# Two blocks instead of one ahead of the expert loop in the second mixture layer, with GpSimd making their low halves

## Chip, cores and metric

The kernel runs on one core of a Trainium2 chip. The metric is device time in microseconds (us): the median of the runs. Three runs of the kernel before took 1082.74, 1085.60 and 1086.61 us; the median is 1085.6 us.

## What is computed

A token matrix x (2048 x 256) passes four stages, each behind a layer norm and a residual with a tanh gate: cross attention, mixture of experts, quantised cross attention, mixture of experts. The change touches the last stage only. Cut to what matters:

```python
def _L1_ffn_ref(...):            # E, I, IS = (16, 176, 704), TOP_K = 4
    x = hidden_states.reshape(-1, h)                 # 2048 x 256
    w_dense = _routing_weights(x, router_w)          # softmax over 16 experts, the 4 best kept
    moe_out = _moe_experts(x, gate_w, up_w, down_w, w_dense)
    shared = jax.nn.silu(x @ shared_gate_w.T) * (x @ shared_up_w.T) @ shared_down_w.T
    shared = jax.nn.sigmoid(x @ se_gate_w.T) * shared
    return (moe_out + shared).reshape(b, s, h)
```

Every token goes through its four experts (the routed part) and through one shared expert of width 704 (the shared part). The two parts are independent until they are added.

## The kernel before

All engine queues are written out by hand, so the order of the work is the order of the program text on each engine, and semaphores alone tie the engines together (`s_h`, `s_hh` and so on; a wait is `at_least(engine, semaphore, base, n)`). `ffn_pe`, `ffn_act`, `ffn_dve` and `ffn_pool` hold one mixture layer's part of TensorE, ScalarE, VectorE and GpSimd; `l` is 0 for the first mixture layer and 1 for the second, which is the only one whose order changes.

**Shared work** is cut into 24 items (`NSH`): 4 blocks of 512 tokens (`BLK`), times 6 chunks of the inner width (`KSH`: five of 128 and one of 64). One item `s` is a chain over four engines: `shared_gate_up(s)` on TensorE (12 matmuls of 512 columns, 6 in the narrow chunk), `shared_silu` on ScalarE (L761), `shared_product` on VectorE (L839, into `wk1`), `shared_high` on ScalarE (L767, the fp16 high half, into `wkh`), `shared_low` on VectorE (L846, the fp16 rest: `wk1` minus `wkh`, into another part of `wkh`), `shared_down` on TensorE (L679, 12 matmuls of 256 columns). `shared_down(s-2)` stands behind `shared_gate_up(s)`. The six items of a block add up in two PSUM banks (4 and 5); `shared_out(b)` on VectorE (L815, four instructions) adds the block to `x_sb` and so frees the banks (`s_accr`).

**Where the items stand.** `HALF = KSH`, so in each mixture layer 6 items (block 0) stand ahead of the expert loop and 18 items (blocks 1 to 3) behind it. The ones ahead are interleaved, one per step `s`, with the routing: `route_part_dve` and `route_part_pe` do at step 0 to 3 the choice of an expert (`choose_dve`), then weights, bases, slots, then at steps 7 to 10 `rows_dve` (one-hot tables, L550, L551, L553), whose products `list_pe` (L386) adds up on TensorE one step later, and at step 12 `list_dve`, which writes the token numbers `ids` (L565, `r_ids`). With `ids` written, `ffn_pool` gathers the rows of 256 slots per group `g` by two indirect DMAs (L631), for 40 groups, at most four groups ahead (`XR`).

**Expert loop.** `group(base, s)` does one group of 256 slots per step on TensorE: transposes of the gathered rows (L703, into PSUM banks 4 and 5, the shared accumulators' banks, so they wait for `s_accr`), gate and up, a transpose, down. The output goes to a DRAM table `ys`.

**Behind the loop** GpSimd gathers for each of the 16 token tiles four rows of `ys` (`gather_rows`, L656: 64 indirect DMAs, at most four tiles ahead of `combine`, by `c_used`). VectorE's loop there has one step `i` per shared item: `shared_out` at `i` = 8, 14 and 20, `shared_product`, `shared_low`, and `combine(i-2)` (L825, L828), in this order. SyncE then stores each finished tile to `out`.

```python
            for s in range(max(HALF + 3, FIRST_STEPS[l])):
                if s == LIST_STEP[l] - 1:
                    shared_out(0)
                route_part_dve(dve, l, s)
                if s < HALF:
                    shared_product(s)
                if 1 <= s < HALF + 1:
                    shared_low(s - 1)
```

## Time and profile before

| | us |
|---|---|
| median of 3 runs (lowest, highest) | 1085.60 (1082.74, 1086.61) |
| the profiled execution's own time | 1080.46 |
| span of its trace | 1078.7 |
| TensorE busy in the span | 847.4 |
| VectorE busy | 751.3 |
| GpSimd busy | 644.2 |
| ScalarE busy | 460.8 |
| mean granted TensorE clock | 0.828 of full speed |

The span runs from the first to the last instruction; 1.8 us of the execution lie outside it. Positions below are us from the start of the span. In a row of the timeline the first number is the start, the second the duration (of several instructions with "x", from the first to the last), and the bracket behind it tells how long the engine had been idle and what ended that; "remote" there means that the releaser isn't seen. In the granted clock 1.00 is 2.4 GHz and 0.50 is 1.2 GHz.

### The profile page before, as it was taken

The page shows a single profiled execution, that of the slowest core. Times are in us where ns is not written, and L with a number is a line of the kernel's source. Part 1 is how long each engine was busy: PE and PEld are TensorE (multiplying, and loading weights), DVE is VectorE, ACT ScalarE, POOL GpSimd, SP SyncE. Part 2 cuts the span into 40 slices and gives each one's busy share as a digit, 9 for nine tenths or more (in the row PEclk, how much of TensorE's full clock was granted, in tenths as well). Part 3 has the DMA queues.
Part 4 walks back from the last instruction along what each step waited for, and adds up shares of the span by engine and source line. Part 5 has one row for each costly group of instructions (what it writes and reads, how often), then busy time and mean ns, then how long its engine had stood idle before and what let it go on. Part 6 is the DMA issues. An engine that isn't in the chain of part 4 may idle for free.

```text
span 1078.7 us, 21036 instructions
## 1 busy us (share of the span) xinstructions
PE 847.4 (79%) x6928; PEld 569.6 (53%) x6929; DVE 751.3 (70%) x1527; ACT 460.8 (43%) x993; POOL 644.2 (60%) x851
## 2 busy tenths in 40 slices
PE   4379667699989777777777787858679999993785
PEld 1267445477645445545445455545557777761442
DVE  5788668466576777798787787947847676751564
ACT  3455243233223356667656666824023333320121
POOL 4597780766285778888888887610054444426752
PEclk9699859799999866687787686758579999996887
DMA  7021142345221100000110000010034444423331
GB/s 250 26 79 40 47 132 57 97 138 158 94 81 49 47 22 11 12 22 22 28 53 13 16 4 2 2 57 22 6 97 127 136 125 136 126 87 99 113 96 56
DMA packets 55444, 75.04 MB, mean 70 GB/s; under 512 B 11068, under 2 KB 46656, under 8 KB 55360
## 3 DMA queue, kind: packets, MB, share of 16 engines
q1 hardware_dynamic: 44992, 44.82, 13.0%
q0 software_dynamic: 10368, 29.14, 10.0%
q8 instruction: 48, 0.79, 0.3%
q14 instruction: 36, 0.29, 0.1%
HBM read 51.45 MB, written 22.49 MB: 69 GB/s over the span
## 4 chain that ended last, share of the span: by engine, by line
PE 39%; POOL 16%; DVE 14%; issue 10%; ACT 6%; DVEq 5%; POOLq 4%; another core or an unknown queue 4%; DMA 2%; SPq 0%; ACTq 0%
PE PS L256 23%; PE PS L679 3%; DVE sb_slotv L1303 2%; PE PS L1188 2%; POOL sb_xnf L631 2%; POOL sb_wk L1606 2%; PE PS L703 2%; PE PS L732 2%; PE PS L1178 2%; ACT sb_wk L1262 1%; POOL sb_region L1412 1%; POOL sb_wkh L1606 1%; POOL sb_xnf L656 1%; PE PS L1099 1%
## 5 line engine op out<-in xcount | busy, mean ns | idle before, releaser
L631 POOL DMA_INDIRECT sb_xnf<-token_table,sb_ids x120 | 115.8, 965 | 181.3 <-DVE sb_ids L565 87.1
L256 PE MATMUL PS<-sb_region,sb_wkh 88*128 (+1 forms) x1440 | 210.8, 297 | 6.1 <-DVE sb_wa L886 2.9
L1303 DVE TENSOR_REDUCE sb_slotv<-PS 128x1 f32<-128x512 f32 x256 | 163.7, 681 | 44.3 <-PE PS L1178 44.3
L256 PEld LDWEIGHTS PS<-sb_region,sb_wkh 88*128 88x128 f16 (+1 forms) x1440 | 138.2, 99 | 57.0 <-issue 12.2
L656 POOL DMA_INDIRECT sb_xnf<-slot_table,sb_place x96 | 96.8, 1008 | 85.1 <-DMA slot_table<-sb_wa 39.2
L256 PE MATMUL PS<-sb_xnT,sb_sgu 128*128 128x512 f16 x528 | 131.5, 398 | 7.7 <-issue 6.5
L679 PE MATMUL PS<-sb_sdn,sb_wkh 128*128 128x256 f16 (+1 forms) x576 | 77.6, 288 | 42.9 <-DVE sb_wkh L846 34.2
L1262 ACT ACTIVATE sb_wk<-PS,sb_slotv 128x512 f32<-128x512 f32 x128 | 86.9, 686 | 37.3 <-DVE sb_slotv L1303 33.4
L761 ACT ACTIVATE sb_wk<-PS 128x512 f32<-128x512 f32 (+1 forms) x48 | 28.6, 596 | 172.0 <-PE PS L256 105.5
L679 PEld LDWEIGHTS PS<-sb_sdn,sb_wkh 128*128 128x128 f16 (+1 forms) x576 | 56.6, 102 | 68.2 <-DVE sb_wkh L846 43.3
L1606 POOL TENSOR_SCALAR sb_wk<-sb_wk 128x512 f32<-128x512 f32 x128 | 79.5, 621 | 21.4 <-ACT sb_wk L1262 12.6
L256 PEld LDWEIGHTS PS<-sb_xnT,sb_sgu 128*128 128x128 f16 x528 | 52.3, 101 | 72.2 <-issue 22.8
L839 DVE SCALAR_TENSOR_TENSOR sb_wk<-PS,sb_wk 128x512 f32<-128x512 f32 (+1 forms) x48 | 33.2, 692 | 80.4 <-ACT sb_wk L761 64.8
L1308 DVE TENSOR_SCALAR sb_wkh<-PS 128x1024 f16<-128x1024 f16 x112 | 76.6, 684 | 10.7 <-PE PS L1200 10.1
L780 ACT ACTIVATE sb_wkh<-PS 128x512 f16<-128x512 f32 x60 | 35.8, 597 | 109.7 <-PE PS L703 102.3
L875 DVE SCALAR_TENSOR_TENSOR sb_wk<-PS,sb_sm,sb_wk 128x176 f32<-128x176 f32 x120 | 42.6, 396 | 51.4 <-ACT sb_wk L789 47.7
L1188 PE MATMUL PS<-sb_idh,sb_wk 128*128 128x128 f16 x512 | 58.5, 269 | 10.6 <-DVE sb_wkh L1308 5.5
L859 DVE TENSOR_TENSOR sb_wkh<-PS,sb_wkh 128x512 f16<-128x512 f32 x60 | 41.4, 691 | 34.9 <-ACT sb_wkh L780 33.5
L789 ACT ACTIVATE sb_wk<-PS 128x352 f32<-128x352 f32 x60 | 27.8, 463 | 86.5 <-PE PS L256 73.1
L1188 PEld LDWEIGHTS PS<-sb_idh,sb_wk 128*128 128x128 f16 x512 | 39.6, 120 | 38.8 <-issue 31.5
L1262 ACT ACTIVATE sb_wkh<-PS,sb_slotv 128x512 f32<-128x512 f32 x64 | 43.4, 682 | 30.9 <-DVE sb_slotv L1303 29.1
L1412 POOL TENSOR_TENSOR sb_region<-sb_stg,sb_region 128x704 f16<-128x704 f32 (+1 forms) x32 | 43.5, 1359 | 20.8 <-issue 19.8
(281 smaller groups left out, 1808.3 us busy)
## 6 DMA issues: line engine op xcount, KB each, us to landing
slot_table<-sb_wa SPq DMA_DIRECT2D x60, 256.0 KB
sb_stg<-gu SPq DMA_DIRECT2D x24, 352.0 KB, 3.0
sb_stg<-dn SPq DMA_DIRECT2D x24, 176.0 KB
token_table<-sb_xnf SPq DMA_DIRECT2D x16, 256.0 KB, 3.7
sb_stg<-sgu SPq DMA_DIRECT2D x8, 352.0 KB, 6.5
sb_x_sb<-x SPq DMA_DIRECT2D x1, 2048.0 KB, 12.2
out<-sb_x_sb SPq DMA_DIRECT2D x16, 128.0 KB
sb_xnf<-token_table,sb_ids POOLq DMA_INDIRECT x120
```

The lines of the kernel that those rows point to most:

```text
L256: last = nc.tensor.matmul(out_, lhs(i, c), rhs(j, c), start=(c == 0 and n == 0 and not begun), stop=(c == C - 1 and n == 2 and not more))
L631: nc.gpsimd.indirect_dma_start(xg[l][:, 2 * (g % XR) + n, :], None, xw[l][:, :], bass.IndirectOffsetOnAxis(ap=ids[:, 2 * g + n:2 * g + n + ...
L656: nc.gpsimd.indirect_dma_start(yr[l][r][:, k, :], None, ys[l][:, :], bass.IndirectOffsetOnAxis(ap=place[:, k, t:t + 1], axis=0))\
L679: last = nc.tensor.matmul(PS[:, 4 + i // 2, i % 2 * D:(i % 2 + 1) * D], wkh[0:r, HR * h + v, i * P:(i + 1) * P], sdn[0:r, j, k, :], start= ...
L859: nc.vector.tensor_tensor(wkh[:, 2 * (s % 2) + 1, :], PS[:, 4 + s % 2, :], wkh[:, 2 * (s % 2), :], ALU.subtract).then_inc(e_xl[l].sem, 1)
L875: last = nc.vector.scalar_tensor_tensor(wk1[:, 2 + u, n * EI:(n + 1) * EI], PS[:, 2 * u + n, EI:EG], wv[u][:, n:n + 1], wk1[:, u, n * EI:( ...
L1188: last = nc.tensor.transpose(bank[:, (h * KT + k) * P:(h * KT + k + 1) * P], h_p[s % NE][:, h, k * P:(k + 1) * P], idh[:, :])
L1262: nc.scalar.activation(h_e[s % NE][:, h, :], PS[:, 2 * u + h, :], ACT.Exp, bias=h_nb[u][:, h:h + 1], accum_out=o_sum[v][:, head:head + 1]) ...
L1303: nc.vector.tensor_reduce(h_nb[u][:, h:h + 1], PS[:, 2 * u + h, :], AX, ALU.max, negate=True).then_inc(h_max, 1)
L1308: nc.vector.tensor_scalar(h_T[s % 2], PS[:, 4 + s % 2, :].bitcast(F16), -RB, None, ALU.add).then_inc(h_pc_dve, 1)
L1412: nc.gpsimd.tensor_tensor(lo, w, hi, ALU.subtract).then_inc(stg_split[n % 4], 1)
L1606: nc.gpsimd.tensor_scalar(h_e[s % NE][:, h], h_e[s % NE][:, h], 255.0, MAGIC + RB_BITS, ALU.mult, ALU.add).then_inc(h_int, 1)
```

## The change

`HALF` becomes a pair, `AHEAD = (KSH, 2 * KSH)`: the first mixture layer keeps 6 items ahead of its loop and 18 behind it, the second has 12 and 12. The second layer's routing loop runs 15 steps on VectorE and 14 on TensorE instead of 13. The first `shared_out` of that layer moves from step 11 to step 8, and a second one is added behind `list_dve`. The low halves of the 12 items ahead go from VectorE (L846) to GpSimd, with a semaphore of their own, `s_lowp`: ten ahead of the first gather, one behind the gathers of group 0, one behind those of group 1. VectorE's loop behind the expert loop is lengthened past its last item, so that the 16 combines fit.

```diff
-        HALF = KSH
+        AHEAD = (KSH, 2 * KSH)
...
+        s_lowp = sem("s_lowp")
...
         LIST_STEP = tuple(2 * k + 4 for k in TOPK)
-        FIRST_STEPS = tuple(max(HALF + 2, n + 1) for n in LIST_STEP)
+        OUT_STEP = (LIST_STEP[0] - 1, KSH + 2)
+        FIRST_STEPS = tuple(max(a + 2, n + 1) for a, n in zip(AHEAD, LIST_STEP))
...
+            def shared_low(s):
+                r = P if s % KSH < SFULL else SREM
+                at_least(pl, s_hh[l], 0, s + 1)
+                at_least(pl, s_d[l], 0, s + 1 - HR)
+                nc.gpsimd.tensor_tensor(wkh[0:r, HR + s % HR, :], wk1[0:r, 2 + s % 2, :], wkh[0:r, s % HR, :],
+                                        ALU.subtract).then_inc(s_lowp, 1)
+
             if l == 0:
                 split_items(pl, 0, FIRST_ITEMS)
+            else:
+                for s in range(AHEAD[1] - 2):
+                    shared_low(s)
             at_least(pl, r_ids[l], 0, 1)
...
             for g in range(NG[l]):
                 gather(g)
+                if l == 1 and g < 2:
+                    shared_low(AHEAD[1] - 2 + g)
...
-                at_least(pe, s_hl[l], 0, s + 1)
+                if l == 1 and s < AHEAD[1]:
+                    pe.wait_ge(s_lowp, s + 1)
+                else:
+                    at_least(pe, s_hl[l], 0, s + 1 - l * AHEAD[1])
...
-            at_least(pe, s_h[l], 0, HALF)
-            at_least(pe, s_accr[l], 0, HALF // KSH)
+            at_least(pe, s_h[l], 0, AHEAD[l])
+            at_least(pe, s_accr[l], 0, AHEAD[l] // KSH)
...
                 at_least(dve, s_silu[l], 0, s + 1)
                 at_least(dve, s_hh[l], 0, s - 1)
+                if l == 1 and 2 <= s < AHEAD[1] + 2:
+                    dve.wait_ge(s_lowp, s - 1)
...
-            for s in range(max(HALF + 3, FIRST_STEPS[l])):
-                if s == LIST_STEP[l] - 1:
+            for s in range(max(AHEAD[l] + 3, FIRST_STEPS[l])):
+                if s == OUT_STEP[l]:
                     shared_out(0)
                 route_part_dve(dve, l, s)
-                if s < HALF:
+                if s < AHEAD[l]:
                     shared_product(s)
-                if 1 <= s < HALF + 1:
+                if l == 0 and 1 <= s < AHEAD[l] + 1:
                     shared_low(s - 1)
+            if l == 1:
+                shared_out(1)
...
             dve.drain()
+            if l == 1:
+                dve.wait_ge(s_lowp, AHEAD[1])
             low_x(0, 0)
...
-            for s in range(HALF, NSH + 3):
-                i = s - HALF
-                if i >= KSH + 2 and (s - 2) % KSH == 0:
+            for s in range(AHEAD[l], max(NSH + 3, AHEAD[l] + 2 + (NT if l == 1 else 0))):
+                i = s - AHEAD[l]
+                if i >= KSH + 2 and s < NSH + 3 and (s - 2) % KSH == 0:
                     shared_out((s - 2) // KSH - 1)
```

In all other places `HALF` becomes `AHEAD[l]`. Line numbers behind the changed places move by 1 to 23: L631, L679, L703, L815, L825, L828, L839, L846 and L386 are L633, L696, L720, L832, L842, L845, L858, L865 and L388 in the changed kernel.

The order on GpSimd at the start of the second mixture layer, before the change (L1679 makes the layer norm's factor, L631 gathers for the expert loop):

```order
L1679 TENSOR_TENSOR sb_rstd<-sb_ve,sb_mhalf 128x16 [waits stats_ready]
L631 DMA sb_xnf<-token_table,sb_ids 128x272 [waits wstored,zeroed1,stored,r_ids]
L631 DMA sb_xnf<-token_table,sb_ids 128x272 x7
L631 DMA sb_xnf<-token_table,sb_ids 128x272 [waits e_h]
L631 DMA sb_xnf<-token_table,sb_ids 128x272
```

and after it (L641 is the low half):

```order
L1702 TENSOR_TENSOR sb_rstd<-sb_ve,sb_mhalf 128x16 [waits stats_ready]
L641 TENSOR_TENSOR sb_wkh<-sb_wk,sb_wkh 128x512 [waits s_hh] x4
L641 TENSOR_TENSOR sb_wkh<-sb_wk,sb_wkh 128x512 [waits s_d,s_hh]
L641 TENSOR_TENSOR sb_wkh<-sb_wk,sb_wkh 64x512 [waits s_d,s_hh]
L641 TENSOR_TENSOR sb_wkh<-sb_wk,sb_wkh 128x512 [waits s_d,s_hh] x4
L633 DMA sb_xnf<-token_table,sb_ids 128x272 [waits wstored,zeroed1,stored,r_ids]
L633 DMA sb_xnf<-token_table,sb_ids 128x272
L641 TENSOR_TENSOR sb_wkh<-sb_wk,sb_wkh 128x512 [waits s_d,s_hh]
L633 DMA sb_xnf<-token_table,sb_ids 128x272 x2
L641 TENSOR_TENSOR sb_wkh<-sb_wk,sb_wkh 64x512 [waits s_d,s_hh]
L633 DMA sb_xnf<-token_table,sb_ids 128x272 x4
```

Twelve vector operations now stand on a queue that held none here, two of them between gathers.

TensorE's queue from the last list product to the expert loop, before:

```order
L386 MATMUL PS<-sb_wa,sb_xnf 128x80 [waits r_rows]
L386 MATMUL PS<-sb_wa,sb_xnf 128x80 x15
L703 MATMUL PS<-sb_idf,sb_xnf 128x128 [waits s_accr,r_ids,s_h,e_ld0,r_tiles,experts_ready1]
L703 MATMUL PS<-sb_idf,sb_xnf 128x128 x3
```

and after:

```order
L388 MATMUL PS<-sb_wa,sb_xnf 128x80 [waits r_rows]
L388 MATMUL PS<-sb_wa,sb_xnf 128x80 x15
L256 MATMUL PS<-sb_xnT,sb_sgu 128x512 [waits s_h]
L256 MATMUL PS<-sb_xnT,sb_sgu 128x512 x5
L696 MATMUL PS<-sb_sdn,sb_wkh 128x256 [waits s_lowp]
L696 MATMUL PS<-sb_sdn,sb_wkh 128x256 x11
L720 MATMUL PS<-sb_idf,sb_xnf 128x128 [waits s_accr,r_ids,s_h,e_ld0,r_tiles,experts_ready1]
L720 MATMUL PS<-sb_idf,sb_xnf 128x128 x3
```

The pair of L696 rows stands there three times (items 9, 10 and 11). A gate-up and three downs now stand between the list products and the first transpose of the loop, and each of the downs waits for GpSimd; the same goes for the three list products before: before the change they stood back to back, now each has a gate-up and a down behind it.

## Rows read from the trace of the kernel before

**Rows 1.** Busy time by stretch: us, then each engine's busy time, granted clock, DMA.
```profile
core 0: us, PE busy (x) PEld busy (x) DVE busy (x) ACT busy (x) POOL busy (x), PEclk, DMA share, GB/s
...
756.00:780.70 24.70, 17.62 (x102) 13.49 (x101) 21.87 (x45) 1.74 (x3) 0.02 (x1) 0.57 0.03 4
...
788.40:958.90 170.50, 166.38 (x1276) 127.74 (x1276) 116.17 (x280) 62.97 (x119) 70.53 (x75) 0.98 0.41 123
958.90:1078.70 119.80, 79.81 (x414) 41.82 (x414) 54.04 (x97) 20.04 (x36) 64.29 (x64) 0.81 0.31 90
```
**Rows 2.** Timeline of the second mixture layer, end of routing to the loop's first groups.
```profile
756.01 1.48 PE L679 MATMUL PS<-sb_sdn,sb_wkh 128*128 128x256 f16 x12
...
760.69 2.74 PE L679 MATMUL PS<-sb_sdn,sb_wkh 128*128 128x256 f16 x12 [3.20 <-DVE sb_wkh L846]
...
780.19 0.20 DVE L565 CAST sb_ids<-sb_wa 128x80 uint32<-128x80 f32 x1
...
780.68 2.10 POOL L631 DMA_INDIRECT sb_xnf<-token_table,sb_ids  x1 [62.18 <-DVE sb_ids L565]
783.09 0.95 POOL L631 DMA_INDIRECT sb_xnf<-token_table,sb_ids  x1 [0.31 <-issue]
...
785.99 1.09 PE L703 MATMUL PS<-sb_idf,sb_xnf 128*128 128x128 f32 x4 [6.74 <-DMA sb_xnf<-token_table,sb_ids]
...
789.34 3.73 PE L256 MATMUL PS<-sb_region,sb_wkh 128*128 x12
```
**Rows 3.** Chain that ended last, in order of time: start us, us, what.
```profile
776.61 2.66 PE PS L386 x16
...
966.99 1.31 PE PS L679 x12
968.30 2.59 PE PS L256 x12
```
**Rows 4.** Timeline behind the expert loop: gathers on POOL, waits on ACT, last DVE work.
```profile
962.45 0.94 POOL L656 DMA_INDIRECT sb_xnf<-slot_table,sb_place  x1 [21.92 <-DMA slot_table<-sb_wa]
...
996.35 0.60 ACT L761 ACTIVATE sb_wk<-PS 128x512 f32<-128x512 f32 x1 [20.06 <-remote]
...
1000.26 0.94 POOL L656 DMA_INDIRECT sb_xnf<-slot_table,sb_place  x1 [7.35 <-DVE sb_x_sb L828]
...
1028.72 0.60 ACT L761 ACTIVATE sb_wk<-PS 128x512 f32<-128x512 f32 x1 [13.74 <-remote]
...
1032.63 0.94 POOL L656 DMA_INDIRECT sb_xnf<-slot_table,sb_place  x1 [6.67 <-DVE sb_x_sb L828]
...
1058.38 0.95 POOL L656 DMA_INDIRECT sb_xnf<-slot_table,sb_place  x1 [0.30 <-issue]
1060.10 0.60 ACT L761 ACTIVATE sb_wk<-PS 128x512 f32<-128x512 f32 x1 [12.56 <-remote]
...
1073.11 1.66 DVE L815 SCALAR_TENSOR_TENSOR sb_x_sb<-PS,sb_sgate,sb_x_sb 128x256 f32<-128x256 f32 x4 [1.64 <-PE PS L679]
```
**Rows 5.** Groups of instructions from 690 us to the end: count, busy us, mean ns.
```profile
L839 DVE SCALAR_TENSOR_TENSOR sb_wk<-PS,sb_wk 128x512 f32<-128x512 f32 (+1 forms) x24 | 16.6, 692 | 59.4 <-ACT sb_wk L761 46.5 <-issue 12.5 <-ACT sb_wkh L767 0.2
L846 DVE TENSOR_TENSOR sb_wkh<-sb_wk,sb_wkh 128x512 f16<-128x512 f32 (+1 forms) x24 | 16.3, 680 | 0.0
...
L828 DVE SCALAR_TENSOR_TENSOR sb_x_sb<-sb_xnf,sb_tga,sb_x_sb 128x256 f32<-128x256 f32 x32 | 15.5, 485 | 2.4
...
L825 DVE TENSOR_TENSOR sb_xnf<-sb_xnf 128x512 f32<-128x512 f32 x16 | 10.9, 683 | 0.8 <-DMA sb_xnf<-slot_table,sb_place 0.8
```
**Rows 6.** Timeline of GpSimd's and VectorE's two-operand work in the attention and first mixture stages.
```profile
421.73 1.15 POOL L1412 TENSOR_TENSOR sb_region<-sb_stg,sb_region 88x512 f16<-88x512 f32 x1 [0.17 <-issue]
...
162.93 1.52 POOL L1412 TENSOR_TENSOR sb_region<-sb_stg,sb_region 128x704 f16<-128x704 f32 x1
...
163.35 1.25 DVE L457 TENSOR_TENSOR sb_wa<-sb_wa,sb_sm 128x128 f32<-128x128 f32 x1
...
166.75 0.29 DVE L473 TENSOR_TENSOR sb_ex<-sb_ex,sb_selm 128x128 f32<-128x128 f32 x1
```

More of the change, by code:

```diff
@@ L687, in ffn_pe @@
                 route_part_pe(pe, l, s)
-                if s < HALF:
+                if s < AHEAD[l]:
                     shared_gate_up(s)
-                if 2 <= s < HALF + 2:
+                if 2 <= s < AHEAD[l] + 2:
                     shared_down(s - 2)
@@ L746, in ffn_pe @@
             at_least(pe, e_h[l], 0, NG[l])
-            for s in range(HALF, NSH + 2):
+            for s in range(AHEAD[l], NSH + 2):
                 if s < NSH:
                     shared_gate_up(s)
-                if s >= HALF + 2:
+                if s >= AHEAD[l] + 2:
                     shared_down(s - 2)
                 if l == 0:
-                    ahead_pe(pe, s - HALF)
+                    ahead_pe(pe, s - AHEAD[l])
             pe.drain().then_inc(shared_used, 1)
@@ L767, in shared_high @@
                 nc.scalar.activation(wkh[0:r, s % HR, :], wk1[0:r, 2 + u, :], ACT.Copy).then_inc(s_hh[l].sem, 1)
-            for s in range(HALF + 1):
-                if s < HALF:
+            for s in range(AHEAD[l] + 1):
+                if s < AHEAD[l]:
                     shared_silu(s)
@@ L793, in group @@
                     nc.scalar.activation(wkh[0:EC, 6 - 2 * u, :], PS[0:EC, 6, :], ACT.Copy).then_inc(e_hh[l].sem, 1)
-            at_least(act, s_d[l], 0, HALF)
+            at_least(act, s_d[l], 0, AHEAD[l])
             high_x(0, 0)
@@ L797, in ffn_act @@
             at_least(act, e_d[l], 0, NG[l])
-            for s in range(HALF, NSH + 1):
+            for s in range(AHEAD[l], NSH + 1):
                 if s < NSH:
                     shared_silu(s)
-                if s >= HALF + 1:
+                if s >= AHEAD[l] + 1:
                     shared_high(s - 1)
                 if l == 0:
-                    ahead_act(act, s - HALF)
+                    ahead_act(act, s - AHEAD[l])
         def ffn_dve(dve, l):
@@ L847, in shared_low @@
                                         ALU.subtract).then_inc(s_hl[l].sem, 1)
-            for s in range(max(HALF + 3, FIRST_STEPS[l])):
-                if s == LIST_STEP[l] - 1:
+            for s in range(max(AHEAD[l] + 3, FIRST_STEPS[l])):
+                if s == OUT_STEP[l]:
                     shared_out(0)
                 route_part_dve(dve, l, s)
-                if s < HALF:
+                if s < AHEAD[l]:
                     shared_product(s)
-                if 1 <= s < HALF + 1:
+                if l == 0 and 1 <= s < AHEAD[l] + 1:
                     shared_low(s - 1)
+            if l == 1:
+                shared_out(1)
             def low_x(base, s):
@@ L897, in ffn_dve @@
                     ahead_dve(dve, i)
-                if HALF + 1 <= s < NSH + 1:
+                if AHEAD[l] + 1 <= s < NSH + 1:
                     shared_low(s - 1)
```

## Prediction, made before the changed kernel ran

> **What bounds the kernel now.** I read the table of stretches first, to cut the second mixture layer into stages, then the chain of waits for what ends last in each, then the timeline at the two seams where items are taken out and put in.
>
> Routing ahead of the loop: from 756.0 to 780.7 us VectorE is busy 21.9 of 24.7 us and TensorE 17.6, at a granted clock of 0.57 [rows 1]. TensorE is busy that long only because it is slow: a down takes 1.48 us at 756.0 and 2.74 us at 760.7, after an idle of 3.2 us [rows 2]. VectorE's routing chain bounds this stage, and TensorE has room. In the loop it is the reverse: TensorE 166.4 of 170.5 us [rows 1]. Nothing in it changes.
>
> Behind the loop 119.8 us pass, with TensorE busy 79.8, VectorE 54.0 and GpSimd 64.3 [rows 1]: no engine is full, so waits bound it. There are three freezes. ScalarE's silu waits 20.1, 13.7 and 12.6 us for a gate-up, and each time it goes on within 1 to 4 us after GpSimd's burst of gathers has paused [rows 4]. VectorE stands in `shared_product` meanwhile, so it doesn't combine; GpSimd runs through the tiles it may gather ahead, then idles 7.35 and 6.67 us for `c_used` [rows 4]. So items and gathers take turns. What freezes the gate-up the trace doesn't say; that a burst had run for 10 us or more each time it does.
>
> **Part 1, the tail loses 6 of 18 items.** The structure of its first 12 steps stays the same (both versions start at a block's first chunk), so I let the first two freezes and both idles of GpSimd stand. The third burst of gathers starts at 1032.6 and its last row at 1058.4, ending at 1059.3 [rows 4]. Before, items 18 to 23 were tied into that burst, froze, and were finished behind it, up to VectorE's last `shared_out` at 1073.1 + 1.66 = 1074.8 [rows 4]; the span ends 3.9 us later (the last store). After, the items end near 1041 and what remains is combine behind gather. The last gather lands 1.9 us after its row ends (785.99 less 783.09 + 0.95 = 784.04, at the start of the loop [rows 2]), combine takes 0.68 + 2 x 0.49 and a gap, 1.8 us [rows 5], the store 3.9: 1059.3 + 1.9 + 1.8 + 3.9 = 1066.9. **The tail gains 78.7 - 66.9 = 11.8, say 12 us.** It isn't the work of six items (6 x 3.9 = 23.4 us at 2.59 + 1.31 [rows 3]), since GpSimd's 64 gathers stay: 962.4 to 1059.3 with 14.0 us of idle [rows 4].
>
> **Part 2, routing gets 6 items.** From the third down on (756.0 [rows 2]) TensorE now has 6 downs, 5 gate-ups, 4 list products and the small tile product to do before the list is complete. It is busy enough to keep its clock, so I use the full-clock prices, 1.31 and 2.59 [rows 3]; a list product took 2.66 at half clock [rows 3], 1.33 at full. 7.9 + 13.0 + 5.3 + 0.3 = 26.5, to 782.5. Behind that stand, ahead of `list_dve`, the short gate-up (1.3), its silu (0.6) and product (0.7), since `shared_product(11)` is in front of it in VectorE's queue; then the list itself (1.1: from 776.61 + 2.66 [rows 3] to 780.19 + 0.20 [rows 2]) and 0.7 for semaphores: 786.9. Before it was 780.4. **Plus 6.5 us.** `shared_out(0)` at step 8 costs 1.66 us that it cost at step 11 before; VectorE has slack there now.
>
> **Part 3, low halves on GpSimd.** VectorE gives 6 x 0.68 = 4.1 us and takes 6 products of 0.69, 4.1 us [rows 5]: nothing. The price of a low half on GpSimd isn't in the trace for this shape; the nearest is 1.15 us for 88 x 512 of the same types [rows 6]. TensorE has two steps between a low half and its down, so this latency is hidden. What isn't is the effect on VectorE: a 128 x 128 operation with both inputs in SBUF takes 0.29 us alone and 1.25 us where it began 0.4 us into a GpSimd operation on two inputs, ending just after that did (163.35 + 1.25 = 164.60; 162.93 + 1.52 = 164.45) [rows 6]. The choice of experts, the weights, the slots and the one-hot tables are such operations. Ten low halves of 1.15 stand beside them; between 0 (all fall beside a product, which reads PSUM) and 10 x 0.96 = 9.6 us. TensorE is the bound from about 756 us on and hides part of it, so I take **plus 3 us**. The Trainium skill (SBUF — State Buffer, Who interferes with whom) says that a VectorE instruction with two SBUF inputs contends with a GpSimd instruction that reads SBUF and that the second one fully blocks; the row agrees. It speaks against this change; without it the sum below would be 3 us lower.
>
> **Part 4, between the list and the loop.** Before, `ids` at 780.4, first transposes at 786.0, first expert matmul at 789.3: 8.9 us [rows 2]. Now the transposes need banks 4 and 5, which `shared_out(1)` frees, behind down 11, behind low half 11, behind the gathers of group 1. In a row: 0.3 + 3.35 (the first two gathers [rows 2]) + 1.25 (low half 10 with its gap) + 2.5 (two gathers) + 1.25 (low half 11) + 2.74 (down 11 at half clock, since TensorE idles before it) + 0.1 + 1.9 (`shared_out`, 1.66 and a drain [rows 4]) = 13.4, and 2.7 from the transposes through high and low halves to the first expert matmul = 16.1. **Plus 7.2 us.** The downs of items 9 to 11 wait here, and with them only this start; ScalarE and VectorE have nothing else to do. Group 0 to 3 are gathered by then, so no gather is late.
>
> **Sum.** Front: 6.5 + 3 + 7.2 = 16.7, bounded by 11 (no blocking, down at full clock, the loop's first groups not waiting for rows) and 20. Tail: -12. Together +4.7, which I round down to +4, as the loop's first groups gain a little from rows that are already there. The profiled execution goes from 1080.5 to 1084.5 us; the median stood 5.1 us above it (1085.6), so I forecast **1089.6 us**, +0.4%. A difference under 0.5% (5.4 us) can't be told from none here.
>
> **Rivals.**
> - *A late freeze* (slower, the other side of the bound). The last down, item 23, comes some 8 us into the third burst. If the freeze takes it, VectorE stands at `shared_out(3)`, step 14, in front of four combines until the gathers have drained, at 1060.1, as in the third freeze now. Then 1.8 + 4 x 1.85 + 3.9 = 13.1: the tail ends at 1073.2 and gains 5.5 instead of 12. With the front at +16: 1096. It decides if the down comes over 10 us into the burst; for it speaks that no burst as long as this one has passed without a freeze, against it that the earliest began some 10 us in. Chance 0.15.
> - *Only one freeze.* If the second doesn't come, GpSimd saves an idle of 6.7 us and the tail 19 in all: +16 - 19 = -3, 1082.6, and with the front at its lower bound 1077.6. For it: freezes have no seen cause, and all items behind the loop could end by 1030. Against: the bursts stay as dense. Chance 0.25, half of it below -0.5%.
> - *The front is cheap.* Blocking costs nothing and the start overlaps better: +11 - 12 = -1, 1084.6. Chance 0.15.
> - *No freeze at all.* 64 gathers in 82 us from 962.4, then 7.6: the tail ends at 1052 and gains 26, with the front -10: 1075. Chance 0.03.
> - The forecast holds the rest, 0.42; a quarter of it is over +5.4 us, as is all of the first.
>
> **Numbers.** Faster by over 0.5%: 0.12 + 0.03 and part of the cheap front, where it meets an easier tail, 0.05: 0.20. Slower: 0.15 + 0.10 and a front near its upper bound, 0.07: 0.32. The same: 0.48. The range leaves out the last rival and the upper part of the first: 1077 to 1097.
>
> **What the new profile would show.** The token list ready near 790 us; the first expert matmul near 806, 16 us later than now; TensorE's clock at 1.0 from 756 to 787; single rows of VectorE's choice and tables (L451 to L553 before) 0.5 to 1 us too long beside L641. The expert loop still 170 us. Behind it two waits of over 10 us for a gate-up, not three, and behind the last gather less than 8 us. **Wrong** it would be if the clock fell to half in routing (each item then 7.8 us instead of 3.9: front +25 or more), if the number of freezes changed, or if list and gathers came before 786.

## The result, and the profile after

Nine runs of each kernel on one chip: the changed kernel takes 1091.37 us (median; 1087.22 to 1101.43), the kernel before 1084.53 us (1076.27 to 1087.80). The ratio is **1.0085, 95% interval 1.0052 to 1.0118** (of the means, 1092.9 and 1083.7): slower, by some 9 us. The forecast was 1089.6 us and +0.4%. The microseconds were met within 1.8, but the whole interval lies above the 0.5% that I had called "the same" and given 0.48; slower by over 0.5% had 0.32. On a second chip the changed kernel came out at 1.0155 (1.0110 to 1.0201), see c1 below.

The profiled execution of the changed kernel is the slowest of its nine, 1101.43 us with a span of 1099.7; before's, with 1078.7, is one of the faster ones. So stages are compared, not spans. The routing of the second mixture layer starts at 742.92 us against 732.93: 9.99 us of the difference had gathered ahead of it, in code that both kernels share, and are left out. (Over all fourteen traces of this study, which share that code, routing starts anywhere from 726.7 to 742.9 us.)

| us | before | changed | |
|---|---|---|---|
| first gate-up of the routing to `ids` written | 47.5 | 66.0 | +18.5 |
| `ids` to the first expert matmul | 8.9 | 16.3 | +7.4 |
| first expert matmul to the first gather behind the loop | 173.1 | 171.8 | -1.3 |
| first gather to the last one's start | 95.9 | 95.7 | -0.3 |
| last gather's start to the end | 20.3 | 7.0 | -13.4 |
| sum | | | +11.0 |

Stretches of the changed kernel, which answer to [rows 1] (the first one starts at the same down, 9.6 us later on the clock, and ends with the token list; columns as there):

```profile
765.60:809.20 43.60, 36.47 (x216) 24.34 (x214) 30.23 (x51) 8.76 (x15) 7.01 (x7) 0.88 0.03 4
823.50:993.50 170.00, 165.90 (x1276) 127.29 (x1274) 116.25 (x280) 63.28 (x120) 68.04 (x72) 0.98 0.40 120
993.50:1099.70 106.20, 54.10 (x276) 27.56 (x276) 45.09 (x81) 13.36 (x24) 63.80 (x64) 0.76 0.34 102
```

The loop is what it was. The stage ahead of it took 24.7 us and takes 43.6, with TensorE busy 36.5 of them: it, not VectorE, is now what fills this stage. Behind the loop TensorE works 54 us instead of 80, and GpSimd the same 64.

The end of routing, timeline of TensorE, with VectorE's and GpSimd's rows that it waits for (L388 is a list product, L256 a gate-up, L696 a down, L552 to L555 the one-hot tables, L641 a low half; compare [rows 2]):

```profile
773.81 1.48 PE L696 MATMUL PS<-sb_sdn,sb_wkh 64*128 64x256 f16 x12
...
777.08 0.82 DVE L552 TENSOR_TENSOR sb_wa<-sb_ctxT_hl,sb_slotc 128x1280 f16<-128x1280 f16 x1
777.73 1.19 POOL L641 TENSOR_TENSOR sb_wkh<-sb_wk,sb_wkh 128x512 f16<-128x512 f32 x1 [4.78 <-ACT sb_wkh L784]
777.82 2.17 DVE L553 TENSOR_TENSOR sb_xnf<-sb_ctxT_hl,sb_slotk 128x2048 f16<-128x2048 f16 x1
780.07 0.82 DVE L555 TENSOR_TENSOR sb_wa<-sb_wa,sb_slotm 128x1280 f16<-128x1280 f16 x1
780.95 2.67 PE L388 MATMUL PS<-sb_wa,sb_xnf 128*128 128x80 f16 x16 [5.66 <-DVE sb_wa L555]
...
783.44 5.22 PE L256 MATMUL PS<-sb_xnT,sb_sgu 128*128 128x512 f16 x12
...
788.49 1.47 PE L696 MATMUL PS<-sb_sdn,sb_wkh 128*128 128x256 f16 x12
789.80 2.62 PE L388 MATMUL PS<-sb_wa,sb_xnf 128*128 128x80 f16 x16
792.25 2.77 PE L256 MATMUL PS<-sb_xnT,sb_sgu 128*128 128x512 f16 x12
794.85 1.47 PE L696 MATMUL PS<-sb_sdn,sb_wkh 128*128 128x256 f16 x12
796.16 2.60 PE L388 MATMUL PS<-sb_wa,sb_xnf 128*128 128x80 f16 x16
```

Three things are to be seen. TensorE is done with down 5 at 775.3 and stands for 5.66 us until the first tables are there. Gate-up 8 could have started at 777.0, when the product ahead of it (item 6) was done, and down 6 at 778.9, behind its low half, but both stand behind the list product in the queue. The gate-up that follows takes 5.22 us instead of 2.77: the granted clock went to half at 778.2, inside that idle time, and came back at 788.4. And a list product takes 2.60 to 2.67 us whatever the clock is.

GpSimd between the list and the loop, and what TensorE waits for there:

```profile
809.20 2.10 POOL L633 DMA_INDIRECT sb_xnf<-token_table,sb_ids  x1 [5.44 <-DVE sb_ids L567]
811.60 0.95 POOL L633 DMA_INDIRECT sb_xnf<-token_table,sb_ids  x1 [0.31 <-issue]
812.58 1.16 POOL L641 TENSOR_TENSOR sb_wkh<-sb_wk,sb_wkh 128x512 f16<-128x512 f32 x1
...
816.12 1.16 POOL L641 TENSOR_TENSOR sb_wkh<-sb_wk,sb_wkh 64x512 f16<-64x512 f32 x1
```
```profile
813.79 2.74 PE L696 MATMUL PS<-sb_sdn,sb_wkh 128*128 128x256 f16 x12 [6.05 <-POOL sb_wkh L641]
817.34 2.74 PE L696 MATMUL PS<-sb_sdn,sb_wkh 64*128 64x256 f16 x12 [0.81 <-POOL sb_wkh L641]
822.25 1.94 PE L720 MATMUL PS<-sb_idf,sb_xnf 128*128 128x128 f32 x8 [2.17 <-DVE sb_x_sb L832]
825.26 1.06 PE L256 MATMUL PS<-sb_region,sb_wkh 128*128 x3 [1.07 <-DVE sb_wkh L880]
```

The chain runs as it was summed: low half 11 behind four gathers, down 11 at half clock, the second `shared_out`, the transposes.

Behind the loop, ScalarE's waits for a gate-up and GpSimd's bursts, which answer to [rows 4]:

```profile
997.05 0.94 POOL L670 DMA_INDIRECT sb_xnf<-slot_table,sb_place  x1 [21.91 <-DMA slot_table<-sb_wa]
...
1034.79 0.94 POOL L670 DMA_INDIRECT sb_xnf<-slot_table,sb_place  x1 [7.36 <-DVE sb_x_sb L845]
...
1056.55 0.94 POOL L670 DMA_INDIRECT sb_xnf<-slot_table,sb_place  x1 [1.17 <-DVE sb_x_sb L845]
...
1067.27 0.94 POOL L670 DMA_INDIRECT sb_xnf<-slot_table,sb_place  x1 [6.01 <-DVE sb_x_sb L845]
...
1092.73 0.95 POOL L670 DMA_INDIRECT sb_xnf<-slot_table,sb_place  x1 [0.30 <-issue]
```
```profile
1030.88 0.60 ACT L778 ACTIVATE sb_wk<-PS 128x512 f32<-128x512 f32 x1 [20.68 <-remote]
...
1052.64 0.60 ACT L778 ACTIVATE sb_wk<-PS 128x512 f32<-128x512 f32 x1 [8.35 <-remote]
...
1063.36 0.60 ACT L778 ACTIVATE sb_wk<-PS 128x512 f32<-128x512 f32 x1 [9.60 <-remote]
```

Three freezes still, two of them shorter; GpSimd stands 14.5 us in all (14.0 before), so the gathers take as long as they did, and the last combine stands right behind the last of them.

### The profile page after: what moved, and what is told of

Same layout as the page of the kernel before. It is cut to its first block, busy times and chain, and to the rows that moved or that the text cites. A ratio compares the mean times of both kernels' runs of the same rounds, so it can differ in the third digit from the quotient of the medians.

```text
span 1099.7 us, 21037 instructions
## 1 busy us (share of the span) xinstructions
PE 857.0 (78%) x6928; PEld 576.4 (52%) x6929; DVE 752.4 (68%) x1515; ACT 460.9 (42%) x993; POOL 657.7 (60%) x863
## 3 DMA queue, kind: packets, MB, share of 16 engines
q1 hardware_dynamic: 44992, 44.82, 12.6%
## 4 chain that ended last, share of the span: by engine, by line
PE 37%; POOL 18%; DVE 12%; issue 11%; ACT 5%; POOLq 5%; another core or an unknown queue 5%; DVEq 4%; DMA 2%; SPq 0%; ACTq 0%
PE PS L256 22%; POOL sb_xnf L633 3%; POOL sb_xnf L670 2%; DVE sb_slotv L1326 2%; POOL sb_wk L1629 2%; PE PS L1211 2%; PE PS L720 2%; PE PS L696 2%; PE PS L749 2%; POOL sb_region L1435 2%; PE PS L1201 2%; ACT sb_wk L1285 2%; POOLq L1434 1%; POOL sb_wkh L1629 1%
## 5 line engine op out<-in xcount | busy, mean ns | idle before, releaser
L256 PE MATMUL PS<-sb_region,sb_wkh 88*128 (+1 forms) x1440 | 211.1, 297 | 7.3 <-issue 3.9
L633 POOL DMA_INDIRECT sb_xnf<-token_table,sb_ids x120 | 115.9, 966 | 128.4 <-DVE sb_wk L896 74.3
L256 PEld LDWEIGHTS PS<-sb_region,sb_wkh 88*128 88x128 f16 (+1 forms) x1440 | 137.5, 99 | 59.5 <-issue 15.1
L256 PE MATMUL PS<-sb_xnT,sb_sgu 128*128 128x512 f16 x528 | 132.8, 403 | 5.2 <-issue 4.2
L696 PE MATMUL PS<-sb_sdn,sb_wkh 128*128 128x256 f16 (+1 forms) x576 | 76.5, 285 | 40.1 <-DVE sb_wkh L865 21.8
L696 PEld LDWEIGHTS PS<-sb_sdn,sb_wkh 128*128 128x128 f16 (+1 forms) x576 | 56.4, 101 | 64.4 <-DVE sb_wkh L865 27.5
L256 PEld LDWEIGHTS PS<-sb_xnT,sb_sgu 128*128 128x128 f16 x528 | 52.9, 102 | 70.3 <-issue 21.2
L858 DVE SCALAR_TENSOR_TENSOR sb_wk<-PS,sb_wk 128x512 f32<-128x512 f32 (+1 forms) x48 | 33.2, 692 | 79.9 <-ACT sb_wk L778 64.1
L797 ACT ACTIVATE sb_wkh<-PS 128x512 f16<-128x512 f32 x60 | 35.7, 597 | 95.5 <-PE PS L720 90.6
L1435 POOL TENSOR_TENSOR sb_region<-sb_stg,sb_region 128x704 f16<-128x704 f32 (+1 forms) x32 | 43.7, 1365 | 22.6 <-issue 21.6
```

The costliest lines, as they stand in the source:

```text
L256: last = nc.tensor.matmul(out_, lhs(i, c), rhs(j, c), start=(c == 0 and n == 0 and not begun), stop=(c == C - 1 and n == 2 and not more))
L633: nc.gpsimd.indirect_dma_start(xg[l][:, 2 * (g % XR) + n, :], None, xw[l][:, :], bass.IndirectOffsetOnAxis(ap=ids[:, 2 * g + n:2 * g + n + ...
L696: last = nc.tensor.matmul(PS[:, 4 + i // 2, i % 2 * D:(i % 2 + 1) * D], wkh[0:r, HR * h + v, i * P:(i + 1) * P], sdn[0:r, j, k, :], start= ...
L1435: nc.gpsimd.tensor_tensor(lo, w, hi, ALU.subtract).then_inc(stg_split[n % 4], 1)
```

## The experiments

Two theories of the front. A: the order on TensorE makes the cost; list products, gate-ups and downs fill one queue there, so it matters where they stand and not who makes the low halves. B: GpSimd's low halves block VectorE, whose chain delays the list. And one of the tail: the 64 gathers are its floor, so items behind the loop are nearly free.

The three groups of runs fell on three chips, here called B, C and D. The kernel before takes 1058.6, 1056.2 and 1058.1 us there, 26 to 28 less than in the first runs, whose chip I therefore take for a fourth. Ratios are against the kernel before on the same chip. "List" and "start" are `ids` and the first expert matmul, in us from the routing's first gate-up (before: 47.4 to 47.5, and 56.4 to 56.5, on the first chip, on C and on D); "tail" is the first gather behind the loop to the end. Ratios are of 6 to 12 runs, stages of one trace each: the two traces of the changed kernel differ by 1.3 us in list and start.

| | chip | ratio (95%) | list | start | tail |
|---|---|---|---|---|---|
| changed | first | 1.0085 (1.0052 to 1.0118) | 66.0 | 82.3 | 102.6 (before 116.3) |
| changed (c1) | C | 1.0155 (1.0110 to 1.0201) | 64.7 | 81.0 | 88.2 (before 95.4) |
| low halves on VectorE (e1) | B | 1.0082 (1.0049 to 1.0114) | 64.7 | 73.8 | 88.1 |
| one block ahead, low halves on GpSimd (e2) | B | 0.9984 (0.9950 to 1.0018) | 47.5 | 56.4 | 93.6 |
| low halves 10, 11 ahead of the gathers (e3) | B | 1.0095 (1.0059 to 1.0131) | 66.6 | 75.5 | 89.1 |
| packed order (e4) | B | 1.0020 (0.9992 to 1.0047) | 60.3 | 70.7 | 87.6 |
| packed order again (d2) | D | 1.0026 (0.9998 to 1.0054) | 57.6 | 68.0 | 90.0 |
| before, combines spread (c3) | C | 0.9966 (0.9934 to 0.9999) | 47.6 | 56.5 | 89.6 |
| before, combines spread (d3) | D | 0.9957 (0.9924 to 0.9989) | 47.3 | 56.3 | 90.6 |
| before, two tiles ahead (c4) | C | 1.0017 (0.9980 to 1.0055) | 47.5 | 56.4 | 95.2 |
| before, six items left out (d1) | D | 0.9921 (0.9885 to 0.9957) | 48.3 | 57.2 | 88.9 (before 94.2) |

### e1: low halves back on VectorE

```diff
-                if l == 0 and 1 <= s < AHEAD[l] + 1:
+                if 1 <= s < AHEAD[l] + 1:
                     shared_low(s - 1)
```
with GpSimd's twelve low halves and `s_lowp` taken out.

> The changed kernel with all 12 low halves ahead of the loop back on VectorE (two blocks ahead stay). Counted from the routing's first gate-up, the changed kernel has its token list at 66.0 us and its first expert matmul at 82.3 us (before: 47.5 and 56.4). Theory A, the order on TensorE: from the first one-hot tables on, list products, gate-ups and downs stand in one queue and fill it, so who makes the low halves matters little: list at 63 to 66 us; only the end gets shorter, since downs 10 and 11 no longer wait behind gathers: first expert matmul at 73 to 76 us, time 6 to 9 us under the changed kernel's. Theory B, GpSimd blocks VectorE: VectorE's chain is what delays the list, list under 60 us, first expert matmul under 70 us, time 12 us or more under the changed kernel's.

Measured: list at 64.7, start at 73.8. Both stand inside theory A's bounds; B's "list under 60, start under 70" isn't met. Against e3 on the same chip, which has all twelve low halves on GpSimd, the list comes 1.9 us sooner. Of this, 1.1 us are the last two instructions of the list itself, which in e3 run beside low halves 10 and 11; in the changed kernel these two low halves stand behind the gathers, and 0.9 us are left for the blocking. The idle time ahead of the first list product is 1.47 us here, not 5.66: down 5 ends 2.3 us later, as it waits for VectorE's low halves, and the first tables are there 1.9 us sooner. The time under the changed kernel's can only be told across chips; it is the ratio that counts, and it is 1.0082 on B against 1.0155 on C.

### e2: only the low halves of before on GpSimd

```diff
-        AHEAD = (KSH, 2 * KSH)
+        AHEAD = (KSH, KSH)
```
and all six low halves of the one block in front of the first gather.

> One block ahead of the second loop, as before the change, but its 6 low halves on GpSimd: the price of that part alone. Theory A (blocking small, VectorE gives 0.68 us per low half and gets some 0.5 to 1 us back per low half): list at 46 to 49 us from the first gate-up, time within 2 us of before. Theory B: 6 blockings of 1 us each land on VectorE's chain, which bounds this stage: list at 50 to 54 us, time 3 to 6 us over before.

List at 47.5 as before, ratio 0.9984 with 1 inside: theory A. Six operations of 1.15 to 1.28 us on GpSimd cost nothing that could be seen; what they take from single VectorE rows VectorE gets back, as it no longer makes them (0.68 us each, [rows 5]).

### e3: low halves 10 and 11 ahead of the first gather

```diff
-                for s in range(AHEAD[1] - 2):
+                for s in range(AHEAD[1]):
                     shared_low(s)
```

> The changed kernel with low halves 10 and 11 also ahead of the first gather on GpSimd. The list stays at 66 us. If the stretch between list and loop (16.35 us) is set by the chain low half 11, down 11, second shared_out, as I summed it, the last low half ends 5 us sooner and the stretch falls to 11 to 12 us: time 4 to 5 us under the changed kernel's. If it is set by the gathers instead, it stays at 15 us or more, as the first gather now starts 2.4 us later.

The stretch between list and loop is 8.9 us, from 16.3: 7.4 less, and as long as before the change. That is more than the 5 that I had summed, since the two downs now run back to back, 2.90 us for both where each took 2.74, and are no longer what the start waits for: TensorE's first transposes wait for the gathered rows. Timeline of that stretch:

```profile
796.61 2.26 POOL L641 TENSOR_TENSOR sb_wkh<-sb_wk,sb_wkh 128x512 f16<-128x512 f32 x2 [3.88 <-ACT sb_wkh L782]
...
797.82 2.90 PE L694 MATMUL PS<-sb_sdn,sb_wkh 128*128 128x256 f16 x24 [1.12 <-POOL sb_wkh L641]
...
797.89 1.04 DVE L567 CAST sb_ids<-sb_wa 128x80 uint32<-128x80 f32 x1
...
799.21 2.10 POOL L633 DMA_INDIRECT sb_xnf<-token_table,sb_ids  x1 [0.34 <-DVE sb_ids L567]
```

The first gather is 0.3 us behind `ids` as ever, but `ids` itself comes late: its cast takes 1.04 us beside a low half, where it takes 0.20 in the changed kernel. The ratio, 1.0095 against c1's 1.0155, points the same way, though across two chips and with intervals that meet.

### e4 and d2: the order behind item 7 packed by hand

```diff
+        PE_REST = (("g", 8), ("g", 9), ("r", 0), ("d", 6), ("r", 1), ("d", 7), ("g", 10), ("r", 2), ("d", 8), ("r", 3),
+                   ("g", 11), ("d", 9), ("d", 10), ("d", 11))
```
(g gate-up, r list product, d down; VectorE's order is written out to match, low halves on VectorE.)

> Low halves on VectorE, and the order behind item 7 written out by hand: gate-ups 8 and 9 stand ahead of the first list product, gate-up 11 and downs 9 to 11 behind the last one, so TensorE has work while VectorE makes the tables and while the first rows are gathered. Theory A (order): TensorE idles under 2 us ahead of the first list product, its clock stays at full, list at 52 to 56 us, first expert matmul at 64 to 67 us from the first gate-up, time 12 to 16 us under the changed kernel's and so 4 to 9 us under before. Theory B (the six items cost TensorE's work wherever they stand, 23.4 us): first expert matmul not under 76 us, time about that of low halves on VectorE alone.

> The packed order (e4) once more, since its expert loop was 6.5 us shorter there than that of the three kernels beside it, which nothing in it explains. If that was the run and not the kernel, the loop takes as long as before's on this chip, the front 14.5 us more, the tail 6 to 7 us less without freezes: ratio 1.005 to 1.010. If the loop is really shorter with it: 1.000 to 1.004.

TensorE of d2:

```profile
775.83 5.35 PE L256 MATMUL PS<-sb_xnT,sb_sgu 128*128 128x512 f16 x24
781.02 2.62 PE L392 MATMUL PS<-sb_wa,sb_xnf 128*128 128x80 f16 x16
783.46 1.49 PE L692 MATMUL PS<-sb_sdn,sb_wkh 128*128 128x256 f16 x12
784.81 2.66 PE L392 MATMUL PS<-sb_wa,sb_xnf 128*128 128x80 f16 x16
...
801.64 2.90 PE L692 MATMUL PS<-sb_sdn,sb_wkh 128*128 128x256 f16 x24 [1.43 <-DVE sb_wkh L862]
```

The idle time ahead of the list product is gone, two gate-ups have taken its place, and the whole row from 775.8 to 800 has no gap. The list of d2 comes 8.4 us sooner than the changed kernel's, and this adds up: from down 5 to the last list product TensorE takes 23.0 us instead of 31.1, with the same work in it, so 8.1 us of idle time and half clock are gone; down 5 starts 2.4 us later, with low halves on VectorE; and the list is written 1.3 us behind the last product instead of 4.0, as it no longer stands behind the short gate-up and its product, 2.6 us. Against the changed kernel the start comes 10 to 14 us sooner (82.3 and 81.0 to 70.7 and 68.0); against e1 on the same chip it is 3.1 us. It missed what I had written for it: start at 68.0 to 70.7, not 64 to 67, because a TensorE that never idles still has 4 list products, 4 gate-ups and 6 downs to do. In e4 the clock fell to half under gate-ups 8 and 9 all the same, which took 7.04 us instead of the 5.35 here, and explains 1.7 of the 2.7 us between the two. So the items cost 12 to 14 us in front in the best order tried, and save 4 to 6 behind. The ratios are nearer to 1 than that. The loop is short in both traces, 161.2 and 161.3 us; in those of the three kernels beside e4 it takes 167.5 to 167.7, on chip C 161.6 to 162.0, on chip D 160.7 to 167.6. With that the stages add up to +1.9 us (e4 against e2) and +2.1 (d2 against before), where the ratios give 2.1 and 2.8, and the ratio of d2 falls into the branch of "really shorter". But the loop was seen in one run of each only, and kernels whose loop is the same show both lengths. Whether the packed program has the short loop for a reason or by luck stays open.

### c1 and c2: both kernels on one more chip

No edit.

> The changed kernel once more, beside the kernel before on the same chip as the others of this group. On the chip of the second group of runs the 64 gathers behind the loop ran without a pause (81 us from first to last, where the first chip took 96), so the tail had no freezes and giving it fewer items is worth 5 to 6 us, not 13. Theory A (front cost fixed by the order, tail gain hangs on the freezes): ratio 1.008 to 1.010 where the gathers of before pause twice, 1.010 to 1.014 where they don't. Rival: the gain of the tail is the same on any chip, and so is the ratio, 1.0085.

> The kernel before, for its profile on this chip: first gather behind the loop to last start 81 us and 12 to 13 us from there to the end if this chip shows no freezes, 96 and 20 if it does; list at 47.5 us and first expert matmul at 56.3 us from the routing's first gate-up on either.

Front +24.6 us (+25.9 on the first chip), loop the same, tail 88.2 against 95.4: -7.2, where the first chip had -13.6. Sum 17.1 us, measured 16.4 (1.0155 of 1056.2). The rival, one ratio for all chips, falls; my own range for a chip without freezes, 1.010 to 1.014, was a little low. End of the tail of before on chip C:

```profile
1036.49 1.72 POOL L656 DMA_INDIRECT sb_xnf<-slot_table,sb_place  x1 [0.30 <-issue]
```
```profile
1040.11 0.69 DVE L825 TENSOR_TENSOR sb_xnf<-sb_xnf 128x512 f32<-128x512 f32 x1 [2.73 <-DMA sb_xnf<-slot_table,sb_place]
1040.88 1.04 DVE L828 SCALAR_TENSOR_TENSOR sb_x_sb<-sb_xnf,sb_tga,sb_x_sb 128x256 f32<-128x256 f32 x2
1041.84 0.68 DVE L846 TENSOR_TENSOR sb_wkh<-sb_wk,sb_wkh 64x512 f16<-64x512 f32 x1
1044.95 1.66 DVE L815 SCALAR_TENSOR_TENSOR sb_x_sb<-PS,sb_sgate,sb_x_sb 128x256 f32<-128x256 f32 x4 [2.44 <-PE PS L679]
```

No freeze here: GpSimd's queue has no gap from the first gather to the last (81.1 us). What remains ahead of the end is plain order: the last combine waits for its gather, and the last low half, down and `shared_out` stand behind that combine.

### c3 and d3: the kernel before, with its combines spread

```diff
+        COMBINE_STEPS = tuple(-(-(128 * t + 180) // 100) for t in range(NT))
...
-                if l == 1 and 2 <= i < 2 + NT:
-                    combine(i - 2)
+                if l == 1 and i in COMBINE_STEPS:
+                    combine(COMBINE_STEPS.index(i))
```
`combine(t)` stands at step 2, 4, 5, 6, 7, 9, ... 21, where its rows land, instead of t + 2.

> The kernel before with one thing changed: behind the loop, combine(t) stands at the step at which its gathers land (5 us per tile against 3.9 us per item) instead of two steps behind item t. Theory: where there are no freezes, items wait for combines that wait for gathers, so the items end 12.5 us behind the last gather's start; now they end before it and 7 us are left: 4 to 6 us faster than before. Where there are freezes they take their time as before and the gain is 0 to 6 us. Rival: the items are slow for another reason (instruction supply), and nothing changes.

> The kernel before with the combines spread over VectorE's steps (c3) once more: ratio 0.993 to 0.998 again, end 7 us behind the last gather's start. If it comes out at 1.000 or more, the gain of c3 was scatter.

0.9966 and 0.9957: 3.6 and 4.5 us faster than before, with both intervals below 1, the first only just (0.9999). The end behind the last gather's start is 6.95 us in both, from 14.2 and 12.4. The rival (nothing changes) falls. VectorE's end in c3, where the last `shared_out` stands two combines ahead of the end:

```profile
1040.72 1.66 DVE L816 SCALAR_TENSOR_TENSOR sb_x_sb<-PS,sb_sgate,sb_x_sb 128x256 f32<-128x256 f32 x4
...
1050.08 1.04 DVE L829 SCALAR_TENSOR_TENSOR sb_x_sb<-sb_xnf,sb_tga,sb_x_sb 128x256 f32<-128x256 f32 x2
```

The tail of c3 is 5.8 us shorter than before's on that chip, where the change takes 7.2 off it (d3: 3.6 us on D), and nothing is paid in front. It is the fastest complete kernel of this study.

### c4: GpSimd at most two tiles ahead

```diff
-            at_least(pl, c_used[l], 0, t + 1 - CR)
+            at_least(pl, c_used[l], 0, t + 1 - (CR if l == 0 else 2))
```

> The kernel before with GpSimd at most two tiles ahead of combine behind the second loop, not four, so a burst of gathers that nothing answers is 8 long (10 us), not 16. If a freeze lasts until the burst pauses, waits for a gate-up fall from up to 20 us to under 12 on a chip with freezes, and the time goes down by 0 to 8 us there. Rival: freezes last as long whatever the gathers do, and the shorter lead only costs, 3 to 10 us. Without freezes: 0 to 4 us slower.

Chip C has no freezes, so this couldn't tell what it was made for. 1.0017, with 1 inside the interval: no cost of the shorter lead is seen there.

### d1 and d4: the last six items left out

```diff
+        ITEMS = (NSH, NSH - KSH)
...
-            for s in range(HALF, NSH + 2):
-                if s < NSH:
+            for s in range(HALF, ITEMS[l] + 2):
+                if s < ITEMS[l]:
                     shared_gate_up(s)
```
and so on the other engines. The shared part of the last 512 tokens isn't computed.

> The kernel before with the last block's six items (18 to 23) left out altogether behind the second loop, so 512 tokens of the output lack their shared part. This is the change's gain in the tail without its cost in front. Theory (the 64 gathers are the floor, 81 us from the first to the last one's start, and 7 us behind them): the time falls by 5 to 8 us on a chip without freezes and by 11 to 14 us on one with them, though the items are 23.4 us of TensorE's work. Rival: TensorE's work behind the loop counts in full there, and the time falls by 20 us or more.

> The kernel before, for its profile on this chip, so that loop, gathers and end can be compared: list at 47.5 us and first expert matmul at 56.2 us from the routing's first gate-up as on the two chips seen; gathers 81 us and 12 to 14 us to the end without freezes, 96 and 20 with them.

Six items fewer, 23.4 us of TensorE's work, and the tail is 88.9 us instead of 94.2: 5.3 less. The time falls by 8.4 us (0.9921, 4.5 to 12.2), a little over the 5 to 8 expected; in these two traces the loop, which has no item in it, differs too, 160.7 against 166.6. The rival, 20 us or more, falls. The tail of the changed kernel on chip C is as long, 88.2 us: without freezes, 64 gathers and 7 us behind them are what is left whether the six items stand elsewhere or nowhere. That is worth 5 to 7 us on such a chip, and the changed kernel pays 25 us for it.

## Why the prediction was right in its number and wrong in its steps

**Part 2, the six items in routing, is the step that failed.** It gave +6.5 us, and with part 3 +9.5 up to the list; it was +18.5. The sum ran over TensorE alone, "busy enough to keep its clock", from the down at 756.0 (down 3, the fourth) to the last list product at 782.5: 26.5 us. The same stretch now runs from 765.6 to 805.1, 39.5 us, and the 13.0 us come apart as follows.
- *TensorE does idle.* 5.66 us ahead of the first list product. I had counted work and not looked at what stands behind the waiting instruction on its queue: gate-up 8, ready from 777.0, and down 6, ready from 778.9, behind a product that waits for VectorE. Packing the order takes this idle time away (d2). Some 1.9 us of it are part 3 and not the order: VectorE's first tables come that much later than in e1, where it isn't blocked.
- *The clock falls once*, in that idle time, and is at half under gate-up 8: 5.05 us to the next down instead of 2.6, 2.4 us. I had named this as what would make the forecast wrong (front +25 or more). The front was +25.9, above the 20 that I had as its bound, but through all three of these and not through the clock alone.
- *The list product was mis-sized.* I took it as 1.33 us at full clock, half of the 2.66 of [rows 3]. It takes 2.45 us to the next instruction at either clock: 4 x 1.12 = 4.5 us. The first two products of the changed kernel, busy time by stretch (the number behind POOL's is the granted clock), with the end of the idle time ahead of them:

```profile
778.00:780.95 2.95, 0.00 (x0) 0.00 (x1) 2.82 (x2) 0.00 (x0) 0.91 (x1) 0.54 0.00 0
780.95:783.40 2.45, 2.45 (x16) 2.36 (x17) 2.21 (x5) 0.00 (x0) 0.00 (x0) 0.50 0.00 0
789.80:792.20 2.40, 2.40 (x18) 2.32 (x17) 2.40 (x3) 0.01 (x1) 1.18 (x1) 1.00 0.00 0
```

What it does follow is its moving columns. The first mixture layer makes its list the same way, at full clock and with 40 columns per matmul where the second has 80. From the trace of the kernel before, timeline of its first list product and of the weight loads (PEld) of this one and of the last of the second layer:

```profile
179.89 1.30 PEld L386 LDWEIGHTS PS<-sb_wa,sb_xnf 128*128 128x128 f16 x16 [0.93 <-DVE sb_wa L553]
179.90 1.49 PE L386 MATMUL PS<-sb_wa,sb_xnf 128*128 128x40 f16 x16 [0.66 <-DVE sb_wa L553]
...
776.61 2.32 PEld L386 LDWEIGHTS PS<-sb_wa,sb_xnf 128*128 128x128 f16 x16 [0.44 <-DVE sb_wa L553]
```

With 40 columns the 16 matmuls start 82 to 85 ns apart, with 80 columns 152 to 156 ns, at full clock and at half, over all fourteen traces. A gate-up's column costs 0.42 ns at full clock (2.59 us for 12 x 512), a column of the list 1.9 to 2.1 ns at either clock. It isn't the weight loads that bound it: one takes some 148 ns in both layers, and where they start 83 ns apart they overlap. Both operands of a list product are one-hot tables, read with a stride of 16 elements; that the stride makes the difference wasn't tried. So there were rows at full clock to read, 1.45 us from 179.90 to the next down for half as many columns, and 1.33 us for all of them couldn't be right.

The Trainium skill (TensorE: Matmul & The Clock Gate, LDWEIGHTS) gives the time of a weight load by its columns alone, with no clock in it; for 128 columns that makes an estimate of 107 ns. The trace agrees neither on the size nor, as a rule, on the clock: a down's loads take 98 ns at full clock and 151 at half (medians of 226 and 61, before), while the list's take 148 at both.

12.6 of the 13.0 us are these three. Behind them the tail of the list took 3.8 us, where 4.4 had been summed. The 3 us that I had added for part 3 are spent within the 13.0, so the list came 9 us later than forecast.

**Part 3, GpSimd blocks VectorE: right as a mechanism, too dear.** Single rows are as long as foreseen, 2.17 us instead of 1.22 for L553 beside the low half at 777.73; nine rows of routing are 0.3 to 1.0 us too long. But the price was 1.9 us on the list with twelve low halves ahead of it (e3 against e1), 0.9 of it with the order of the changed kernel, and none with six (e2), where I had +3. (One trace each, and the changed kernel's own two lists are 1.3 us apart.) VectorE gives up a low half of 0.68 us for each that GpSimd makes, and from 781 us on it has slack.

**Part 4, between list and loop: right.** 16.3 us against 16.1, by the chain that was written down, and e3 shows that it is that chain: without the gathers in front of low halves 10 and 11 it is 8.9, as before the change.

**Part 1, the tail: right on the chip it was read from.** It gains 13.6 us, not 12; the idle time of GpSimd stayed (14.5 for 14.0), and the end behind the last gather is 7.0 us for the 7.6 summed. The freezes weren't the two of over 10 us that I expected but one of 20.7 and two of 8.4 and 9.6: "items and gathers take turns" held, the number didn't. Nor does a burst have to run for 10 us first: in the trace of before the first silu that is late, by 4.3 us, belongs to a gate-up that ended 8.4 us into the burst. On the other chips this part is worth 5 to 7 us, because nothing freezes there. My rival of fewer freezes had the sign of its effect wrong for this reason: it counted only what the changed kernel would save. The kernel before saves more, and the change comes out worse, 1.0155.

**The late freeze**, the rival on the slower side, did not come: the last down's `shared_out` ends at 1079.2, four combines ahead of the end.

So front and tail were 25.9 and 13.6 in place of 16.7 and 12, and with the loop 1.3 us shorter the sum is +11.0 instead of +4.7. The median moved by 6.8 us between two samples of nine that each spread over 11 us or more, and the median of before came out 1.1 us under the one that I had started from. That the forecast in microseconds looks better than its steps were is luck.

## What to carry to other kernels

Work moved from a stage with a floor of its own (here 64 gathers at 1.25 us) saves only what stands behind the floor: take items away altogether in one run before moving them, and first try to order what stands behind. Work moved into an in-order queue is priced by that queue as it stands, with each wait and what is ready behind it, not by summing its busy time. Before halving a duration for the clock, look for the same instruction at the other clock elsewhere in the trace: here the first mixture layer had it.

## What the runs showed of the hardware that was not expected

- The same program takes 1084.5 us on one chip and 1056 to 1059 us on three others. 21 to 22 us of it are the tail (116.3 against 94.2 and 95.4 us). On the first chip ScalarE began a silu up to 21.6 us behind the end of its gate-up while GpSimd's gathers ran back to back; on the others it is 0.04 to 0.09 us, with the same instructions in the same order. In the trace of before, the gate-up whose silu starts at 996.35 [rows 4]:

```profile
972.04 2.75 PE L256 MATMUL PS<-sb_xnT,sb_sgu 128*128 128x512 f16 x12
```

And a gate-up of the same kernel on chip C, with its silu:

```profile
976.67 2.75 PE L256 MATMUL PS<-sb_xnT,sb_sgu 128*128 128x512 f16 x12
...
979.46 0.60 ACT L761 ACTIVATE sb_wk<-PS 128x512 f32<-128x512 f32 x1 [3.59 <-PE PS L256]
```

The waits of 10 to 12 us for a gate-up that are left on the other chips are another thing: TensorE stands for `shared_out`, which stands behind a combine, 5.93 us in one piece in e2. Why ScalarE starts late wasn't found, nor whether it is the chip or the occasion, as all traces with freezes are of the first runs; c4, meant for it, fell on a chip that doesn't freeze.

- The expert loop of the same kernel took 162.0 us in one trace and 166.6 in another (first to last expert matmul, before on chips C and D). On C each group behind the third takes 3.98 us. On D they do so up to the ninth; from there to near the end every fourth takes 4.4 to 4.5 us and the others 4.0 to 4.1. Gaps of 0.2 to 0.3 us on TensorE that the profile puts down to issue are 1.3 us of the 4.6; the rest wasn't found.
- The granted clock fell to half even where TensorE had not idled for longer than 1.5 us in the 10 us before. In e1 it fell in the first list product and gate-up 8 behind it took 5.26 us; in e4 it fell at the start of gate-up 8, and gate-ups 8 and 9 together took 7.04 us, while in d2, the same program, it stayed at full and they took 5.35.
- A matmul of the list with its 80 columns, read with a stride of 16 elements, takes 152 to 156 ns at full clock and at half, where a gate-up goes from 2.6 to 5.1 us.
